# The gate's softmax in a float32 graph network: reciprocal multiplied in on TensorE, minimum in place of maximum

## The reference

```python
def _L3_gnn_ref(x, adj_matrix, W_qk, W_v):
    qk = jnp.einsum('bnd,ed->bne', x, W_qk)
    q, k = jnp.split(qk, 2, axis=-1)
    v = jnp.einsum('bnd,ed->bne', x, W_v)
    scores = jnp.einsum('bnd,bmd->bnm', q, k) * inv_scale
    w = jnp.sum(scores * adj_matrix, axis=-1, keepdims=True)
    w = jax.nn.softmax(w, axis=1)
    return w * v
```

## Time and profile before

| what | us |
|---|---|
| median of 3 runs | 1309.1 |
| lowest and highest | 1306.83, 1310.12 |
| the profiled execution | 1306.8 |
| its span, first to last instruction | 1305.0 |
| PE busy, weight loads busy | 1286.8, 1183.3 |
| VectorE busy | 1201.8 |
| ACT busy | 911.5 |
| GpSimd busy | 139.8 |

### The profile page before, as it was taken

How to read it: one execution, slowest core, us unless ns; L and a number is a source line. 1 busy time by engine, 2 the same in 40 slices (tenths; PEclk the granted TensorE clock), 3 DMA queues, 4 the chain that set the end, 5 groups by cost and what they waited for, 6 DMA issues and landing times.

```text
span 1305.0 us, 30579 instructions
## 1 busy us (share of the span) xinstructions
PE 1286.8 (99%) x10987; PEld 1183.3 (91%) x10987; DVE 1201.8 (92%) x3821; ACT 911.5 (70%) x2445; POOL 139.8 (11%) x265
## 2 busy tenths in 40 slices
PE   8999999999999999999999999999999999999997
PEld 7899999999999999999999999999999999999985
DVE  6898999999999999999999999999999999998996
ACT  5767667677667677676677676776676776776773
POOL 0000110101110101101001101011101011110011
PEclk9999999999999999999999999999999999999999
DMA  5211011110111100111100111101111101110000
GB/s 192 68 34 35 1 43 43 42 42 2 43 42 43 42 26 18 43 42 43 42 16 28 43 42 43 42 2 42 43 42 43 34 11 42 43 42 10 10 10 25
DMA packets 51588, 49.03 MB, mean 38 GB/s; under 512 B 7920, under 2 KB 51184, under 8 KB 51440
## 3 DMA queue, kind: packets, MB, share of 16 engines
q1 hardware_dynamic: 51440, 47.08, 11.8%
HBM read 38.68 MB, written 8.39 MB: 36 GB/s over the span
## 4 chain that ended last, share of the span: by engine, by line
PE 96%; DVE 1%; DMA 1%; ACT 1%; issue 0%; POOL 0%; SPq 0%; POOLq 0%; DVEq 0%; ACTq 0%
PE psum L1473 63%; PE psum L1487 13%; PE psum L1717 9%; PE psum L1679 8%; PE psum L1768 1%; PE psum L1771 1%; DMA adj_sb<-in_adj 1%; PE psum L1780 1%; PE psum L1790 0%; POOL rstd L333 0%; ACT fT_h L373 0%; DVE bn L854 0%; SPq L233 0%; DVE x L888 0%; ACT adj_junk L429 0%
## 5 line engine op out<-in xcount | busy, mean ns | idle before, releaser
L521 ACT ACTIVATE work<-work,shift 128x256 f32<-128x256 f32 x512 | 253.8, 499 | 35.5 <-DVE shift L1017 35.5
L1036 DVE SCALAR_TENSOR_TENSOR work<-work,rsum,extra 128x256 f32<-128x256 f32 x512 | 216.5, 473 | 0.2
L373 ACT ACTIVATE work<-psum 128x512 f32<-128x512 f32 x256 | 138.3, 595 | 76.6 <-PE psum L1487 72.6
L1017 DVE CUSTOM_DVE_ANT_0 work<-psum,minus_big 128x256 f32<-128x256 f32 x512 | 189.3, 416 | 0.9 <-PE psum L1679 0.9
L373 ACT ACTIVATE sup_h<-psum 128x512 fp32r<-128x512 f32 x128 | 75.7, 591 | 156.6 <-PE psum L1473 156.6
L330 POOL TENSOR_TENSOR mv<-mv,eps 128x2 f32<-128x2 f32 x128 | 32.4, 253 | 1151.1 <-DVE mv L875 1151.1
L1473 PE MATMUL psum<-x2T_h,wqkv_h 128*128 128x256 f32 x512 | 145.0, 283 | 0.0
L1473 PE MATMUL psum<-x2T_h,wqkv_l 128*128 128x256 f32 x512 | 142.4, 278 | 0.0
L1473 PE MATMUL psum<-x2T_l,wqkv_h 128*128 128x256 f32 x512 | 142.4, 278 | 0.0
L1487 PE MATMUL psum<-ident,work 128*128 128x128 f32 x1024 | 129.5, 275 | 0.0
L1717 PE MATMUL psum<-work,v_sb 128*64 128x256 f32 x1024 | 124.7, 386 | 0.0
(11 more groups left out here) (134 smaller groups left out, 3753.6 us busy)
## 6 DMA issues: line engine op xcount, KB each, us to landing
xT_sb<-in_xT SPq DMA_DIRECT2D x32, 256.0 KB, 2.7
adjT_sb<-in_adjT SPq DMA_DIRECT2D x32, 256.0 KB, 3.2
adj_sb<-in_adj SPq DMA_DIRECT2D x32, 256.0 KB, 4.7
x_sb<-in_x SPq DMA_DIRECT2D x32, 256.0 KB, 4.8
out<-y_sb SPq DMA_DIRECT2D x32, 256.0 KB, 4.3
work<-in_L_gnn_W_qkv SPq DMA_DIRECT2D x1, 1536.0 KB, 9.2
mask_row<-in_nodemask SPq DMA_DIRECT2D x32, 32.0 KB, 4.5
w_raw<-in_L_gnn_W SPq DMA_DIRECT2D x3, 256.0 KB, 6.3
```

Of the source, the lines that this page charges most:

```text
L373: return nc.scalar.activation(dst, src, ACT.Copy, scale=scale)
L521: last = nc.scalar.activation(prob[:, p % 2, i, h], prob[:, p % 2, i, h], ACT.Exp, bias=shift[:, p % 2, h, i:i + 1], scale=-1.0, accum_out ...
L1017: last = V_.tensor_tensor_reduce(out=prob[:, p % 2, i, h], in0=bank(SCORES[p] + h)[:, i * N:(i + 1) * N], in1=minus_big[:, g % 2, i], scal ...
L1036: last = V_.scalar_tensor_tensor(out=prob[:, p % 2, i, h], in0=prob[:, p % 2, i, h], scalar=rsum[:, p % 2, h, i:i + 1], in1=extra[:, g % 2 ...
```

## The change

The score sums are made with the sign turned (`minus_gate`). VectorE takes their minimum, which is the negated maximum of the scores, and ACT's exponential has scale -1. The row of exponentials is no longer multiplied by the reciprocal on VectorE: PE, in place of transposing the row with a 1x1 identity, multiplies it by the 1x1 reciprocal in two float32 products. Two VectorE instructions a graph, the tensor `one` and its set on GpSimd go.

```diff
-        one = sb("one", [1, 1])
...
-            nc.gpsimd.memset(one[:, :], 1.0)
...
                 nc.scalar.activation(gate_exp[:, :], bank(GATE_ROW)[0:1, 0:N], ACT.Exp, bias=gate_shift[:, :],
-                                     accum_out=gate_sum[:, :]).then_inc(act_gate_exp, 1)
+                                     scale=-1.0, accum_out=gate_sum[:, :]).then_inc(act_gate_exp, 1)
...
-                        in1=qkv3[:, t, 0:D].unsqueeze(1).broadcast_to([P, 2, D]), scale=QK_SCALE, scalar=0.0,
-                        op0=ALU.mult, op1=ALU.add, accum_out=gate[:, t:t + 1])
+                        in1=qkv3[:, t, 0:D].unsqueeze(1).broadcast_to([P, 2, D]), scale=-QK_SCALE, scalar=0.0,
+                        op0=ALU.mult, op1=ALU.add, accum_out=minus_gate[:, t:t + 1])
...
-                V_.tensor_reduce(gate_max[:, :], bank(GATE_ROW)[0:1, 0:N], AX.X, ALU.max).then_inc(dve_gate_max, 1)
-                dve.wait_ge(dve_gate_max, once(g))
-                V_.tensor_scalar(gate_shift[:, :], gate_max[:, :], -1.0, None, ALU.mult).then_inc(dve_gate_shift, 1)
+                V_.tensor_reduce(gate_shift[:, :], bank(GATE_ROW)[0:1, 0:N], AX.X, ALU.min).then_inc(dve_gate_shift, 1)
...
                 V_.reciprocal(gate_rsum[:, :], gate_sum[:, :]).then_inc(dve_gate_rsum, 1)
-                dve.wait_ge(dve_gate_rsum, once(g))
-                V_.tensor_scalar(gate_prob[:, :], gate_exp[:, :], gate_rsum[:, :], None, ALU.mult) \
-                    .then_inc(dve_gate_prob, 1)
...
-                pe.wait_ge(dve_gate_prob, once(g))
+                pe.wait_ge(dve_gate_rsum, once(g))
+                pe.wait_ge(act_gate_exp, once(g))
                 pe.wait_ge(dve_x2_pre, once(g + 3))
-                pe.wait_ge(act_gate_exp, once(g))
                 for t in range(NT):
-                    last = nc.tensor.transpose(bank(GATE_COL)[:, t:t + 1], gate_prob[:, block_of(t)], one[:, :])
+                    last = mm(bank(GATE_COL)[:, t:t + 1], gate_exp[:, block_of(t)], gate_rsum[:, :],
+                              start=t == 0, stop=t == NT - 1)
```

More of the change, by code:

```diff
@@ L117, in graph_blocks_kernel @@
         gate_junk = sb("gate_junk", [P, NT, 2, D])
-        gate = sb("gate", [P, NT])
-        gate_max = sb("gate_max", [1, 1])
+        minus_gate = sb("minus_gate", [P, NT])
         gate_shift = sb("gate_shift", [1, 1])
@@ L123, in graph_blocks_kernel @@
         gate_exp = sb("gate_exp", [1, N])
-        gate_prob = sb("gate_prob", [1, N])
         gate_col = sb("gate_col", [P, NT])
@@ L193, in graph_blocks_kernel @@
          dve_x3_pre, dve_x3T, dve_k3_hi, dve_k3, dve_gate,
-         dve_gate_max, dve_gate_shift, dve_gate_rsum, dve_gate_prob, dve_x4_pre, dve_y) = (
+         dve_gate_shift, dve_gate_rsum, dve_x4_pre, dve_y) = (
             sem(n) for n in ("dve_w", "dve_xT", "dve_adjT", "dve_deg", "dve_rdeg", "dve_adj_sum", "dve_extra",
@@ L197, in graph_blocks_kernel @@
                              "dve_x2_bout", "dve_x2T", "dve_qk", "dve_scores", "dve_rsum", "dve_prob", "dve_oT",
-                             "dve_x3_pre", "dve_x3T", "dve_k3_hi", "dve_k3", "dve_gate", "dve_gate_max",
-                             "dve_gate_shift", "dve_gate_rsum", "dve_gate_prob", "dve_x4_pre", "dve_y"))
+                             "dve_x3_pre", "dve_x3T", "dve_k3_hi", "dve_k3", "dve_gate", "dve_gate_shift",
+                             "dve_gate_rsum", "dve_x4_pre", "dve_y"))
         dve_sup, dve_hid, dve_x = sems("dve_sup", 3), sems("dve_hid"), sems("dve_x", 3)
@@ L1779, in gate_row @@
                 for t in range(NT):
-                    last = nc.tensor.transpose(bank(GATE_ROW)[0:1, t * P:(t + 1) * P], gate[:, t:t + 1], ident[:, :])
+                    last = nc.tensor.transpose(bank(GATE_ROW)[0:1, t * P:(t + 1) * P], minus_gate[:, t:t + 1],
+                                               ident[:, :])
                 last.then_inc(pe_gate_row, 1)
```

## The result

The changed kernel takes 1318.4 us (median of 6 runs, 1316.6 to 1320.5) against 1309.3 us of the kernel before (6 runs): ratio 1.0073, 95% interval 1.0062 to 1.0084, 9.1 us slower. I had predicted 1315.1 us, 6.0 us slower, with a range of 1309.0 to 1319.0. The sign and the mechanism were right and the size was a third too small. The time lies only 0.6 us under the upper end of the range.

A forecast was written before the change was run, and what follows sets the result against it. PE, busy for all 40.00 us of a 40 us stretch, was taken to bound the kernel. Its added loads, +6.3 us, and the end, -0.35, made about +6.0 on 1309.1: 1315.1 us, range 1309.0 to 1319.0.

The forecast's parts named there:

- VectorE, inside the slots: Negation and product leave VectorE in each of 32 graphs, some 16 us in all, costed at nothing inside the slots.
- The cover: VectorE's waits for ACT (0.63 us) and for the last GCN product (0.53 us) soak up the freed time.
- rival A: Freed VectorE time reaches PE at its wait before the scores, whole 5.0 us gone: 1310.1 us; 6%.
- A float32 product is two loads and two products: Gate's transposes on PE: 4 loads and 4 products a graph in place of 2 and 2, line 1790's count 128.
- Rival B: PE's second load and product of each float32 product cost nothing, only the end is left: 1308.6 us; 14%.
- the count of 64: Sign for rival B: line 1790's products stay at 64, a float32 product of one row issued as one pair.
- What one more costs: Gate's products on PE: two added loads at 0.105 each, 0.21 us a graph, 30 x 0.21 = +6.3 us.
- The upper bound: PE's four gate loads with nothing overlapped at 135 ns each: 0.33 us a graph, +9.9 us.
- Rival C: Gate's float32 products cost four times the pair's 0.21, +18.9 us, the end gives nothing: 1328.0 us; 8%.
- The end: Last graph's gate chain: closing sum earlier, set by ACT's copy, not VectorE's queue; -0.35 us (bounds -0.5 and 0).

The follow-up runs named there:

- e1: Changed kernel with PE transposing the exponentials by the 1x1 identity again, division by the sum left out (VectorE's part alone): 1307.8 us, ratio 0.9999 to the kernel before.
- e10: Kernel before with one, gate_max and gate_prob allocated behind all other tensors, no instruction changed: 1310.4 us, ratio 1.0012.
- e3: Kernel before with each of the gate's two transposes issued twice, four in place of two: 1311.0 us, ratio 1.0024.
- e6: Changed kernel with only 64 of the 128 columns of each half loaded, half of the gates left out: 1308.3 us, measured one time.
- e9: Changed kernel with the dropped one, gate_max and gate_prob allocated again in their old places, unused: 1316.0 us, ratio 1.0061 to the kernel before.
- e2: Kernel before with two float32 products with the 1x1 one in place of the two transposes (PE's part alone): 1315.2 us, ratio 1.0057.
- e7: Kernel before with the minimum of negated scores and no negation; VectorE's product and PE's transposes stay: 1307.7 us, ratio 1.0006.

## Why the prediction was right, and where its size was off

*VectorE, inside the slots: worth nothing.* Right; e1 (0.9999) is VectorE's part, and its slot is that of e10, where VectorE works as before. The cover was in part another: the negation's time went where I put it, the product's is soaked up by the third support's low part and not by the GCN sum, whose wait stayed at 14.5 us. The wait before the scores, rival A's 5.0 us, is 4.9.

*A float32 product is two loads and two products.* Right: 128 and 128. Rival B (they cost nothing) and the count of 64 are out.

*What one more costs: this is the step that was off.* "Today's pair takes 0.21 us of the chain, 0.105 each", so four would be 0.42, +0.21 a graph. Measured, the piece is 0.53, +0.32 a graph, and the sum's main term is 30 x 0.32 = 9.6 us in place of 6.3. Two errors stood in it against each other. A part of the pair's 0.21, about 0.09, comes once a piece (e3: 0.33 for four), so a further transpose would have cost 0.06, not 0.105. But a load outside the transpose mode costs 0.11, and that holds for all four, not for the two added ones. I had taken the load of "the same shape"; the shape was the same and the mode was not. The form row of the load had no say in it: 135 ns in the transpose mode, 186 outside. The trace of before held two hints: the adjacency products' 0.10, which I used to confirm the 0.105, are outside the transpose mode, and the pair's two loads start 0.06 apart. The upper bound, four unoverlapped loads at 135 ns, gave +0.33 a graph and so nearly the measured value, by the wrong reason. It is luck that 1318.4 us lies within the range: its upper end rests on this bound alone, and the four loads do overlap (186 ns each, 0.11 apart).

The Trainium skill would have given the load's price: TensorE: Matmul & The Clock Gate, section LDWEIGHTS, divides the columns by 1.2 for nanoseconds, 107 ns for 128 columns and 53 ns for 64. The runs agree outside the transpose mode, 0.11 and 0.057 (e6), and don't inside it, 0.06 for 128; there the measurement decides.

*Rival C, four passes at full price.* Out: the piece is 0.53 and not 0.84 us. The Trainium skill, FP8 and Floating Point Precision, section TensorE Precision Notes, counts four passes for a true float32 product. The trace lists two products for each, and with one moving column they cost no more than their loads do; whether each of them is two passes no run here shows.

*The end.* -0.35 was worked out, 0.40 measured. The copy and not VectorE's queue ends last there, as said.

*Not in the sum.* The 0.05 a slot, 27 x 0.05 = 1.4 us, from the tensors that the change drops. The stretch shows it in every kernel. Of the slot it is 0.05 between e9 and the changed kernel (39.88, 39.94), but 0.03 between the kernel before and e10 (39.58, 39.61). By the times it is hardly to be seen: e9 has 1.0061 against 1.0073, with overlapping intervals, and e10 1.0012, whose interval begins at 1.0001, while its profiled execution took 1306.6 us and that of the kernel before 1306.8.

*The sum with the measured terms.* 9.6 + 1.4 - 0.4 = 10.6 us, where the two profiled executions differ by 1317.5 - 1306.8 = 10.7 and the medians by 9.1 (8.1 to 11.0). The agreement with 10.7 is closer than the terms deserve: a slot grew by 0.36 us and not by 0.32 + 0.05, and 0.5 us of the 10.7 lies ahead of the first piece (138.15 us against 137.66), where the change does nothing on PE. And the medians tell sums of this size only to 1 or 2 us: e2 has the 0.53 us piece in 30 graphs too, and its ratio, 1.0057, is 7.5 us.

No version came out measurably ahead of the kernel before. e7, the minimum without the rest, is the change's one part that costs nothing (1.0006, the interval holds no change) and it gains nothing that can be measured.

## What to carry to other kernels

A transpose on PE and a product of the same shape are not the same price: before one is put in place of the other, count the loads that the product's type makes of it, and price each by a row of the same mode, not only of the same shape. A pair's time in a full queue can have a part that comes once, as here; look how far apart the two start, or repeat the pair, before dividing by two. Work taken from VectorE, busy for 92%, was worth nothing here while PE had 40.00 us in a stretch of 40, and the row that decides this is the busy time by stretch.

## What the runs showed that I had not expected

- A load of 128 columns in the transpose mode costs PE 0.06 us of a full queue, outside it 0.11, and half of the columns half of that. A part of 0.09 us comes once. It is a fit of six pieces (0.21, 0.33, 0.31, 0.53, 0.98, and 0.32 for 64 columns), and the steps between the products' starts put 0.02 of it behind the first product and 0.065 behind the last.
- The place of the tensors in SBUF makes 0.05 us in a stretch of 144 products, with no instruction changed (e10); a slot is 0.03 to 0.05 us longer, 0.1% at most. In so tight a comparison a dropped tensor is a change of its own. That it is the 32 bytes of `one` was not shown by itself.
- The start is the same in all these kernels but for the tensors' places and a set on GpSimd, and still the first gate's piece begins between 135.9 us (e6) and 139.5 us (e7) in the profiles. Differences of the medians under 3 us say little here; the slot by the chain says more.
